# Destination numbers fetched for two edge groups at a time, and seven read-back buffers in place of eight

## The reference

```python
h = x @ W_in + b_in
Wij = ssp(f_ij @ Wf1 + bf1) @ Wf2 + bf2        # f_ij: 20 numbers per edge, ssp = softplus - log 2
Wij = Wij * rcut_ij[:, None]
x_ij = h[idx_j] * Wij                          # idx_j: the edge's destination number
agg = jax.ops.segment_sum(x_ij, idx_i, num_segments=n_atoms)   # idx_i: its source number
out = ssp(agg @ Wo1 + bo1) @ Wo2 + bo2
```

## Time and profile before

| | us |
|---|---|
| median of three timed runs | 1561.71 |
| lowest and highest | 1560.51, 1570.42 |
| span of the profiled execution | 1946.8 |
| from its first scatter to its last | 63.4 to 1498.8 |

### The profile page before, as it was taken

How to read it: one execution, slowest core, us unless ns; L and a number is a source line. 1 busy time by engine, 2 the same in 40 slices (tenths; PEclk the granted TensorE clock), 3 DMA queues, 4 the chain that set the end, 5 groups by cost and what they waited for, 6 DMA issues and landing times. The chain is left out here.

```text
span 1946.8 us, 27953 instructions
## 1 busy us (share of the span) xinstructions
PE 1341.5 (69%) x8978; PEld 1063.8 (55%) x9069; DVE 1324.4 (68%) x2333; ACT 915.5 (47%) x2178; POOL 818.6 (42%) x845
## 2 busy tenths in 40 slices
PE   5676555777777677777677877777766558058775
PEld 4443334456665456665556656666556545058775
DVE  8676555366766566676666767677645459999996
ACT  1444443555656655565555655556542021045442
POOL 3465565555555555555554555555554010000000
PEclk7787777978898878888888888888887866579997
DMA  5221222356653566563655546665554380066551
GB/s 200 76 75 63 86 63 57 94 143 198 184 164 102 160 190 177 166 189 130 177 171 161 158 143 185 185 172 162 154 169 121 96 242 0 0 241 225 178 188 34
DMA packets 246482, 276.35 MB, mean 142 GB/s; under 512 B 35121, under 2 KB 194255, under 8 KB 242996
## 3 DMA queue, kind: packets, MB, share of 16 engines
q1 hardware_dynamic: 196944, 183.66, 30.7%
q10 hardware_dynamic: 23524, 37.35, 8.3%
q0 software_dynamic: 25856, 53.42, 8.1%
HBM read 163.13 MB, written 111.20 MB: 141 GB/s over the span
## 5 line engine op out<-in xcount | busy, mean ns | idle before, releaser
L1862 POOL DMA_INDIRECT edge_rows<-x_rows,pos x808 | 791.3, 979 | 678.3 <-DVE x_rows L1491 423.3
L1376 ACT ACTIVATE h_edge<-ps_wh,w_col 128x128 f32<-128x128 f32 x808 | 229.7, 367 | 345.9 <-remote 241.1
L1212 PEld LDWEIGHTS ps_d<-back_one,back 128*128 128x128 f32 x2070 | 312.4, 234 | 137.8 <-issue 112.4
L1212 PE MATMUL ps_d<-back_one,back 128*128 128x128 f32 x2070 | 325.5, 322 | 64.8 <-DVE agg_t L1685 50.1
L1491 DVE TENSOR_TENSOR x_rows<-ps_wh,h_edge 128x512 f32<-128x512 f32 x202 | 139.0, 688 | 271.1 <-ACT h_edge L1376 110.4
L1007 PE MATMUL ps_wh<-yard 128*128 128x150 bf16 x1575 | 160.0, 251 | 194.1 <-issue 77.4
L1175 PE MATMUL ps_wh<-wf,filt 128*128 128x128 f32 x1616 | 255.5, 304 | 11.5 <-issue 10.2
L1161 PE MATMUL ps_v<-f_t,wf 128*128 128x512 f32 x400 | 256.2, 726 | 4.5 <-issue 4.4
L1007 PEld LDWEIGHTS ps_wh<-yard 128*128 128x128 bf16 x1575 | 124.5, 107 | 245.1 <-issue 182.3
L1175 PEld LDWEIGHTS ps_wh<-wf,filt 128*128 128x128 f32 x1616 | 223.2, 212 | 14.1 <-issue 10.9
L1487 DVE SCALAR_TENSOR_TENSOR filt<-ps_v,sp_log 128x512 f32<-128x512 f32 x202 | 138.2, 684 | 105.3 <-ACT sp_log L1371 76.3
(11 more groups left out here) (311 smaller groups left out, 1597.0 us busy)
## 6 DMA issues: line engine op xcount, KB each, us to landing
c_tab<-yard SPq DMA_DIRECT2D x25, 1575.0 KB
c_in<-c_tab SPq DMA_DIRECT2D x25, 1575.0 KB, 6.7
dst_bc<-dst ACTq DMA_DIRECT2D x99, 252.0 KB
back<-edge_rows SPq DMA_DIRECT2D x42, 516.0 KB
edge_rows<-x_rows,pos POOLq DMA_INDIRECT x808
back<-edge_rows SPq DMA_DIRECT2D x50, 258.0 KB
back<-edge_rows SPq DMA_DIRECT2D x55, 193.5 KB
m_tab<-yard SPq DMA_DIRECT2D x25, 393.8 KB
```

Source lines behind the costliest of these rows:

```text
L1212: mm = nc.tensor.matmul(acc(c), back[:, n % BR, k0 + t, 0:D], back_one[:, m % 2, o + t, :], start=t == 0, stop=t == k1 - k0 - 1, skip_grou ...
L1376: copy = nc.scalar.activation(h_edge[:, j, q, :], ps_wh[:, bank, 1, q * D:(q + 1) * D], ACT.Copy, scale=w_col[:, t(q)])
L1862: return pool.indirect_dma_start(table[s], bass.IndirectOffsetOnAxis(places_here, 0), rows, None)
```

## The change

`dst_bc` becomes twice as large, two slots of two groups each. ACT loads a pair of groups with one transfer of 4096 bytes per partition, at every fourth half step (k % 4 == 1), where it loaded one group of 2048 bytes at every second. SP loads the first pair with one transfer in the stage before. The semaphores `dst_in` count pairs. To make room, `back` has seven buffers, and with BR the plan of the read-backs changes too. The branch `more_windows`, which isn't taken with these inputs, is adapted.

```diff
-BR = 8
+BR = 7
...
-        dst_bc = held("dst_bc", [P, 2, WG], I16)
+        dst_bc = held("dst_bc", [P, 2, 2, WG], I16)
...
-                for i in range(2):
-                    sp.dma_start(dst_bc[0:3 * WN, i, :],
-                                 dst16[i * WG:(i + 1) * WG].partition_broadcast(3 * WN)).then_inc(dst_in[i], 16)
+                sp.dma_start(dst_bc[0:3 * WN, 0, :, :].rearrange("p u e -> p (u e)"),
+                             dst16[0:2 * WG].partition_broadcast(3 * WN)).then_inc(dst_in[0], 16)
...
-                def load_dst(i):
-                    act.wait_ge(onehot_done, 2 * i - 2)
-                    act.dma_start(dst_bc[0:3 * WN, i % 2, :],
-                                  dst16[i * WG:(i + 1) * WG].partition_broadcast(3 * WN)).then_inc(dst_in[i % 2], 16)
+                def load_dst(p):
+                    act.wait_ge(onehot_done, 4 * p - 4)
+                    n = min(2, NG - 2 * p)
+                    act.dma_start(dst_bc[0:3 * WN, p % 2, 0:n, :].rearrange("p u e -> p (u e)"),
+                                  dst16[2 * p * WG:(2 * p + n) * WG].partition_broadcast(3 * WN)).then_inc(dst_in[p % 2], 16)
...
-                            if k % 2 and k + 4 < NH:
-                                load_dst(k // 2 + 2)
+                            if k % 4 == 1 and k + 3 < NH:
+                                load_dst((k + 3) // 4)
...
-                    dve.wait_ge(dst_in[i % 2], (i // 2 + 1) * 16)
+                    dve.wait_ge(dst_in[i // 2 % 2], (i // 4 + 1) * 16)
...
-                    onehot(j, i % 2, slice(i, i + 1), slice(0, 1)).then_inc(onehot_done, 1)
+                    onehot(j, i % 4, slice(i, i + 1), slice(0, 1)).then_inc(onehot_done, 1)
```

More of the change, by code:

```diff
@@ L1090, in more_windows @@
                 def more_windows():
+                    sp.wait_ge(dst_in[0], 16)
                     for j in range(2):
                         sp.wait_ge(f_in[j], 16)
-                        sp.wait_ge(dst_in[j], 16)
                         sp.wait_ge(win_in[j], 16)
@@ L1102, in more_windows @@
                         sp.dma_start(f_t[0:RBF, 0, :], a["f_t"][:, at]).then_inc(g_in, 16)
-                        sp.dma_start(dst_bc[0:3 * WN, 0, :], dst16[at].partition_broadcast(3 * WN)).then_inc(g_in, 16)
+                        sp.dma_start(dst_bc[0:3 * WN, 0, 0, :], dst16[at].partition_broadcast(3 * WN)).then_inc(g_in, 16)
                         first = value(sp, ctrl[0:1, bass.ds(i, 1)], NP - WN)
@@ L1481, in onehot @@
                 def onehot(j, u, i, w):
-                    return nc.vector.tensor_scalar(onehot_t[:, j, :], dst_bc[0:3 * WN, u, j * HALF:(j + 1) * HALF],
+                    return nc.vector.tensor_scalar(onehot_t[:, j, :], dst_bc[0:3 * WN, u // 2, u % 2, j * HALF:(j + 1) * HALF],
                                                    base_p[0:3 * WN, i], win_off[0:3 * WN, w], ALU.subtract,
```

## The result

| | before | after |
|---|---|---|
| median of four timed runs, us | 1563.08 (1560.51 to 1570.42) | 1589.17 (1579.08 to 1592.12) |
| ratio of the times | | 1.017, 95% interval 1.0138 to 1.0202 |
| its profiled execution: time, span | see below | 1588.52, 1586.4 |

The change makes the kernel 26 us slower. It was forecast at 1568, within 1% of before; the time lies 10 us above the upper end of the range.

What follows compares the result with a forecast made beforehand. The prediction took POOL's scatters, 5.08 us per half step, to bound the loop, and DVE, PE and transfers the tail. Terms 0 + 0 + 5 + 1.5 = +6.5 on 1561.7 gave 1568 us, range 1552 to 1579.

Steps and rivals of the forecast that it cites:

- The loop is POOL's: Edge loop: unprofiled it runs at POOL's scatter pace, 1026 us of about 1050, 5.08 us per half step.
- Where the earlier trace came from: Edge loop: nearly all of POOL's waits, 423.3 us for DVE's products, exist in the profiled execution and not in timed runs.
- Seven buffers, in the loop: Edge loop: windows 142 and 163 stall DVE 4.8 us each, mostly absorbed by POOL's rows; +1.5 us, bounds 0 and 9.6.
- Seven buffers, in the tail: Tail behind the loop: one buffer fewer lengthens the steps between PE's sets; +5 us, from 1 to 6.4.
- the two next-set windows: Tail, windows 182 and 192, read by the very next set: steps of 7.1 us instead of 4.97, 2 us for both.
- the missing early windows: Tail: windows DVE now does while waiting are missing once in two sets, 0.67 us each, 3.0 us in all.
- Fewer issues on ACT: Loop, ACT: 49 fewer load issues remove 18.1 us from a path that sets no pace; 0, bounds 0 and -18.1.
- A transfer twice as large: Loads of `dst_bc`: the larger transfer lands in 4 to 6 us and stays covered; cost 0.
- the late read-backs aren't absorbed in the loop: Rival, half steps 185 to 201: POOL has under a half step of rows in hand; 1585 us, chance 0.10.

Runs made afterwards that it cites:

- The new profile of before: The kernel before, run again unchanged for a new profile: 1565.25 us, ratio 0.9995; its profiled execution took 1565.78 us.
- the two later occasions: Later timings in which every kernel took some 1940 us; the unchanged kernel before took 1942 and 1946 us.
- the late stalls: Kernel before, with DVE repeating its product six times in each of half steps 180, 182, 184, 186 and 188: 1581.11 us, ratio 1.014.
- The plan alone: Kernel before with eight buffers and waits of eight, but read-backs issued by the plan of seven: 1572.94 us, ratio 1.0074.

## Why the prediction was wrong

**The loop is POOL's: right for nine tenths of it.** The scatters need 1026 us and the loop of before takes 1052. But the conclusion "5.08 us per half step, whatever the other engines do" was used for the last tenth too, where DVE is the slower: half steps 178 to 193, with rows in hand at 1.00. DVE's 4.99 us are those of one half step in mid-loop; in half steps 160 to 177 it is busy 5.13 to 5.18. The rise could have been read from the profile at hand: there DVE is busy 101.7 us in half steps 140 to 159 (1042.12 to 1191.16), 5.09 each, and 52.9 in 160 to 169 (1191.16 to 1264.51), 5.29 each.

**Where the earlier trace rows came from: wrong.** The waits of 423.3 us were put down to the profiler. The new profile of before shows 60.3 us for the same line, and the profiled run takes what the timed ones take; the 1946.8 us were a condition in which the timed runs can be as well, as on the two later occasions. The loop's length in the timed runs was worked out rightly all the same, but that profile couldn't show where POOL is out of rows, since it is so everywhere in it. The prediction saw this ("it waits everywhere there") and still chose absorption.

**Seven buffers, in the loop: the step that failed.** "POOL, however, has up to three half steps of rows in `x_rows`, 15 us, and half steps 193 to 195 ... fill them." At 180 to 192 it has none beyond those just made, so a stall of DVE goes to the time at once, which the late stalls show (22.9 of 21.8 us by half step 189). The term was +1.5. It is 12.2 us at the last scatter plus 6.5 of arrears behind it, 18.7 with the pair transfer's gain in it, and 19 (12 to 26) in the kernel whose loop alone waits as with seven. A second part of the step fell too: only windows 142 and 163 were priced, at 4.8 us each, the other 21 moves of the plan at nothing. DVE waits 4.4 and 2.5 us for these two, but before waits 4.3 us in the set of 142 as well. The growth stands at two of the 21, windows 138 and 149, for which before doesn't wait: 6.4 and 5.7 us. DVE goes on with them 8.4 us behind their issue (1038.48 to 1046.85, 1071.12 to 1079.52), where 4.0 had been taken for issue and landing; why they take so long stays open. The plan alone costs 12.

**Seven buffers, in the tail: the mechanism right, the size low.** +5 was forecast, by steps of 4.97 growing to 5.5, with two steps near 7. The nine sets grow by 5.4 us between the two traces, but by 8 (5 to 12) in the kernel whose tail alone waits as with seven, and before's 45.1 is the longest of its kind. That 5.4 is so near to 5 is luck in part: the two next-set windows were put at 2 us together and their steps grow by 5.1 (1.9 and 3.2), and the missing early windows were put at 3.0 and the six other steps together grow by 0.3. Within the nine sets DVE's waits for read-backs grow from 13.5 to 17.2 us, the longest from 3.0 to 5.6; an increase of 5 was forecast.

**Fewer issues on ACT: 0 taken, 5 measured.** It is inside the bounds of 0 and -18.1. The gain comes where DVE is behind, since there a product that is earlier is worth something; this place for it is read from the rows in hand of one trace each, not shown by a run of its own.

**A transfer twice as large: right.** No wait of DVE for `dst_bc` stands among after's waits, nor among those of the pairs with eight buffers; the kernel that issues at every half step has one, of 2.2 us.

**The rival that came true** is the third, "the late read-backs aren't absorbed in the loop", with its place (185 to 201; after has 1.00 at 178 to 194), its condition (less than a half step in hand) and its price, 1585 against 1589. It had 0.10. Its split is off: it has 9.6 us for windows 142 and 163 and 1.5 each for 138 and 149. The condition could have been weighed from rows at hand: even DVE's 4.99 us against POOL's 5.08 leave 0.09 us per half step to build a stock from, and what is once taken from it comes back slowly. From half step 160 on nothing is left to build it from, as DVE's busy time shows. That sets of ten tiles instead of seven begin at half step 188 keeps it empty by the same reckoning, which no run tried.

## What to carry to other kernels

Before counting on a buffer between two engines to absorb a stall, count what lies in it at that place: producer's rows finished less consumer's rows started, step by step. A ring of four that holds two or three steps in mid-loop may be empty near the end, where the producer has more work per step, and a stall there is paid at once. An average over the loop doesn't show this; the producer's busy time per step in each stretch does. A resource that is traded away (here a buffer worth 34 us for a transfer worth 5) is priced at the place where it is shortest, and its arrears are followed into the next stage.

## What the runs showed of the hardware

**The granted clock inside the tail.** The view by windows of after over single sets of 20 matmuls each (the eighth column is the granted clock):

```profile
1174.41:1178.90 4.49, 4.49 (x20) 4.31 (x20) 1.93 (x7) 0.00 (x0) 0.00 (x0) 0.52 0.00 0
1179.79:1182.26 2.47, 2.47 (x20) 2.28 (x20) 0.05 (x1) 0.00 (x0) 0.00 (x0) 1.00 0.49 133
1186.29:1190.90 4.61, 4.61 (x20) 4.32 (x20) 0.96 (x3) 0.00 (x0) 0.00 (x0) 0.50 0.00 0
```

The sets behind 5.09 and 4.03 us of idle PE run at half clock, 1.2 GHz, and take about 4.5 us; the set behind 0.87 us runs at 2.4 GHz and takes 2.47. It isn't so each time: the last set of after, behind 0.87 us, takes 2.90 for 12 matmuls where before takes 1.58. So a wait for a read-back in the tail can be followed by a set that takes up to 2.1 us longer (4.61 against 2.47). The prediction took 2.47 for every set. This isn't what the change costs in the tail: the first eight sets take PE 29.0 us in after and 29.1 in before.

**Pauses that overlap on all engines.** In the execution of the earlier trace rows all engines stand still now and then, at overlapping times. From its timeline:

```profile
613.10 0.42 DVE L1685 TENSOR_TENSOR agg_t<-ps_d,agg_t 128x256 f32<-128x256 f32 x1 [4.49 <-remote]
613.16 1.14 ACT L1376 ACTIVATE h_edge<-ps_wh,w_col 128x128 f32<-128x128 f32 x4 [5.28 <-remote]
...
616.16 0.97 POOL L1862 DMA_INDIRECT edge_rows<-x_rows,pos  x1 [4.69 <-issue]
```

DVE stands still for 4.49 us, ACT for 5.28, PE for 3.47 and POOL for 4.69, and from 611.47 to 613.10 all four do. Waits put down to "remote", as here, are among the longest of the view of waits in the execution of 1946.8 us (241.1 us on ACT's `h_edge` alone) and do not stand in that of 1565.78. What brings them about these runs don't show.
